# Dense expert layers: the share is applied by ScalarE on eviction, VectorE sums one tile later

## What is computed

```python
logits = jnp.einsum('bsd,de->bse', x, Wr)
w, sel = jax.lax.top_k(logits, 2)
w = jax.nn.softmax(w, axis=-1)
gate = jnp.einsum('bsk,bske->bse', w, jax.nn.one_hot(sel, E, dtype=w.dtype))
for e in range(E):          # E = 8, every expert for every token
    out = out + gate[..., e:e + 1] * (jnp.einsum('bsd,df->bsf', x, We[e]) + be[e])
# x = x + 0.5 * that, of layernorm(x)
```

## Time and profile before

| | us |
|---|---|
| median of 3 runs | 1696.71 (1686.7 to 1700.94) |
| span of the profiled execution | 1695.7 |
| dense layer 0, from its first row addition to its last sum | 963 to 1135 |
| dense layer 1, from its first statistics to its last sum | 1570 to 1693 |

### The profile page before, as it was taken

One profiled execution on the slowest core, in us unless ns is written; L12 is line 12 of the kernel. 1 busy time (PEld: TensorE's weight loads), 2 busy tenths in 40 slices (PEclk: granted clock), 3 DMA queues, 4 the chain that ended last, 5 costly groups with the idle time before them and its releaser, 6 DMA issues. The chain is left out here.

```text
span 1695.7 us, 39494 instructions
## 1 busy us (share of the span) xinstructions
PE 1441.4 (85%) x14334; PEld 990.9 (58%) x14334; DVE 1075.4 (63%) x2743; ACT 750.3 (44%) x1786; POOL 773.8 (46%) x741
## 2 busy tenths in 40 slices
PE   6879999448889996888999478877899999998799
PEld 3556656414545554455566356654677777777687
DVE  6852222457876564783222388876998888874888
ACT  5533333254555633553333311125776666752322
POOL 4453332763320000454333466606998888973000
PEclk9989999569999998899999788888999999999899
DMA  8309995631110002514999232200000000000000
GB/s 265 98 14 267 284 266 150 204 96 38 38 38 1 1 1 67 152 40 123 280 296 259 73 87 84 78 4 13 3 16 3 12 7 3 16 3 3 10 19 22
DMA packets 92664, 145.50 MB, mean 86 GB/s; under 512 B 25032, under 2 KB 52528, under 8 KB 92512
## 3 DMA queue, kind: packets, MB, share of 16 engines
q1 hardware_dynamic: 62816, 93.06, 19.1%
q0 software_dynamic: 15360, 37.77, 7.7%
q10 hardware_dynamic: 14336, 12.59, 2.7%
HBM read 122.39 MB, written 18.87 MB: 83 GB/s over the span
## 5 line engine op out<-in xcount | busy, mean ns | idle before, releaser
L2298 POOL TENSOR_TENSOR sb_m_prob<-sb_m_prob,sb_m_rinv 128x512 f32<-128x512 f32 x256 | 260.1, 1041 | 44.6 <-DVE sb_m_rinv L2348 40.8
L1272 POOL DMA_INDIRECT sb_c_rows<-slot_rows,sb_slot x192 | 192.1, 1000 | 102.7 <-issue 51.2
L2228 ACT ACTIVATE sb_m_prob<-m_ps_s,sb_m_nmax 128x512 f32<-128x512 f32 x256 | 173.8, 683 | 125.8 <-DVE sb_m_nmax L2354 125.2
L1106 POOL DMA_INDIRECT e_xn<-xn_rows,sb_table x128 | 117.7, 920 | 209.6 <-PE e_ps_x L1184 197.2
L1255 DVE TENSOR_TENSOR sb_e_h<-sb_e_sg,e_ps_gu 96x176 f32<-96x176 f32 x128 | 42.6, 333 | 256.5 <-ACT sb_e_sg L1231 256.5
L1193 PE MATMUL e_ps_gu<-e_wgu,sb_e_xT 128*96 128x352 f32 x512 | 178.1, 470 | 17.0 <-ACT sb_e_xT L1225 15.6
L2354 DVE TENSOR_REDUCE sb_m_nmax<-m_ps_s 128x1 f32<-128x512 f32 x256 | 163.8, 681 | 28.1 <-PE m_ps_s L2132 25.7
L2362 DVE STREAM_TRANSPOSE sb_m_pT<-sb_m_prob 128x1024 f32<-128x1024 f32 x128 | 157.5, 1232 | 0.0
L2145 PE MATMUL m_ps_v<-sb_m_pT,sb_m_lat_rows 32*64 32x128 f32 x8192 | 136.1, 275 | 4.6 <-issue 3.8
L2131 PE MATMUL m_ps_s<-sb_m_latT_high,sb_m_qa 128*128 128x512 f32 x256 | 125.5, 490 | 16.0 <-ACT sb_m_prob L2228 15.9
L2145 PEld LDWEIGHTS m_ps_v<-sb_m_pT,sb_m_lat_rows 32*64 32x64 f32 x8192 | 120.2, 131 | 27.8 <-issue 27.4
(11 more groups left out here) (280 smaller groups left out, 3076.4 us busy)
## 6 DMA issues: line engine op xcount, KB each, us to landing
e_wgu<-wgu SPq DMA_DIRECT2D x128, 352.0 KB, 4.9
e_wdn<-wdn SPq DMA_DIRECT2D x128, 192.0 KB, 4.7
slot_rows<-sb_e_y ACTq DMA_DIRECT2D x128, 96.0 KB
xn_rows<-e_xn SPq DMA_DIRECT2D x16, 256.0 KB, 2.2
sb_c_rows<-slot_rows,sb_slot POOLq DMA_INDIRECT x192, 2.8
sb_x<-x SPq DMA_DIRECT2D x4, 512.0 KB, 5.4
e_xn<-xn_rows,sb_table POOLq DMA_INDIRECT x128, 5.3
sb_g_zm<-wqT SPq DMA_DIRECT2D x1, 2048.0 KB, 9.1
```

Of the source, the lines that this page charges most:

```text
L1106: pool.indirect_dma_start(x, None, k.xn_rows[:, :], bass.IndirectOffsetOnAxis(ap=k.table[:, e:e + 1], axis=0))\
L1272: pool.indirect_dma_start(rows[u][j][:, :], None, k.slot_rows[:, :], bass.IndirectOffsetOnAxis(ap=k.slot[:, n, j:j + 1], axis=0))\
L2228: act.activation(prob[s % 4][:, hh, :], ps_s[j % 3][:, :], ACT.Exp, bias=nmax[s % 2][:, hh:hh + 1], accum_out=rsum[s % 2][:, hh:hh + 1]).t ...
L2298: pool.tensor_tensor(part, part, rinv[s % 2][:, hh:hh + 1].to_broadcast([P, T]), ALU.mult)\
```

## The change

The eight expert outputs of a tile are read by ACT instead of DVE. Each is a Copy with the token's share as a scale operand, into one of two buffers `gy[u]` of eight rows of 256 columns (`weigh`, two instructions per pair). ACT's `weigh(n, 0)` now stands first in its tile and waits for `gate_ready`; `inverse_deviation(n+2)` moves behind `weigh(n, 1)`. DVE no longer reads `ps_e`. In tile n it sums the eight rows of tile n-1 by halves (`halve` over 1024, 512 and 256 columns), adds the result to `x` (`add_up`), and adds the bias product of tile n from PSUM to `x` (`add_bias`), which ACT no longer copies. Before the gate of tile n is written, DVE waits until ACT has used up the gate of tile n-2. PE's bias matmul waits for `bias_added`. The last tile is summed after the loop. The loop starts at n = 2, with tiles 0 and 1 written out. The store of a tile waits for one more count of `out_ready`.

```diff
+        gy = [sb(f"d{r}_gated{u}", [P, 2 * NP, D]) for u in range(2)]
...
                 pe.wait_ge(gateT_ready, g + 1)
+                pe.wait_ge(bias_added, g + 1)
                 pe.matmul(ps_b[:, :], gateT[:, :], k.be1[:, :], start=True, stop=True).then_inc(bias_ready, 1)
...
+            def weigh(n, u, j):
+                g = n + r * NT
+                act.wait_ge(pair_ready, g * NP + (j + 1))
+                if j == 0:
+                    act.wait_ge(gate_ready, g + 1)
+                    act.wait_ge(out_ready, g + 1)
+                for i in range(2):
+                    ins = act.activation(gy[u][:, i * NP + j, :], ps_e[j][:, i, :], ACT.Copy,
+                                         scale=gate[u][:, 2 * j + i:2 * j + i + 1])
+                ins.then_inc(pair_free, 1)
...
             def tile(n, u):
                 g = n + r * NT
+                weigh(n, u, 0)
                 if live(n + 1):
                     copies(n + 1, 1 - u)
+                act.wait_ge(gateT_raw, g + 1)
+                act.activation(gateT[:, :], ps_g[:, :], ACT.Copy).then_inc(gateT_ready, 1)
+                weigh(n, u, 1)
                 if live(n + 2):
                     inverse_deviation(n + 2, u)
-                act.wait_ge(gateT_raw, g + 1)
-                act.activation(gateT[:, :], ps_g[:, :], ACT.Copy).then_inc(gateT_ready, 1)
-                act.wait_ge(bias_ready, g + 1)
-                act.wait_ge(out_ready, g + 1)
-                act.activation(acc[:, :], ps_b[:, :], ACT.Copy).then_inc(k.sem("d_bias_copied"), 1)
                 if live(n + 1):
                     gap_exp(n + 1)
+                weigh(n, u, 2)
+                weigh(n, u, 3)
...
+            def halve(n, u, width):
+                g = n + r * NT
+                if width == NP:
+                    dve.wait_ge(pair_free, g * NP + 2 * NP)
+                else:
+                    dve.wait_ge(halved, g * 3 + (1 if width == 2 else 2))
+                part = gy[u][:, 0:width, :]
+                dve.tensor_tensor(part, part, gy[u][:, width:2 * width, :], ALU.add).then_inc(halved, 1)
...
+            def add_bias(n):
+                dve.wait_ge(bias_ready, g + 1)
+                dve.tensor_tensor(x, ps_b[:, :], x, ALU.add).then_inc(bias_added, 1)
+
+            def add_up(n, u):
+                dve.wait_ge(halved, g * 3 + 3)
+                dve.wait_ge(bias_added, g + 2)
+                dve.tensor_tensor(x, gy[u][:, 0, :], x, ALU.add).then_inc(out_ready, 1)
+
+            def tile(n, u):
+                before = not isinstance(n, int) or n > 0
                 add(n + 3, 1 - u, 0)
                 if live(n + 2):
                     normalise(n + 2, u)
                 add(n + 3, 1 - u, 1)
+                if before:
+                    halve(n - 1, 1 - u, 4)
+                add(n + 3, 1 - u, 2)
+                if before:
+                    halve(n - 1, 1 - u, 2)
                 if live(n + 1):
                     leaders(n + 1, 1 - u)
+                if before:
+                    halve(n - 1, 1 - u, 1)
                 add(n + 3, 1 - u, 3)
...
+                rest = [last_sum, lambda: add(n + 3, 1 - u, 4), lambda: add_bias(n), lambda: add(n + 3, 1 - u, 5)]
                 if live(n + 1):
                     gates(n + 1, 1 - u, rest)
...
+            def last_tile_summed():
+                n, u = NT - 1, (NT - 1) % 2
+                for width in (4, 2, 1):
+                    halve(n, u, width)
+                add_up(n, u)
```

## The result

The changed kernel takes 1722.18 us (median; 1713.32 to 1725.81) beside 1694.12 for the kernel before, four runs each: 1.0145 times as long, with a 95% interval of 1.0101 to 1.019. The prediction was 1717 us with a range of 1700 to 1737; of its three cases slower, above 1713.7, came true. The profiled execution after has a span of 1724.0 us, before 1695.7.

The account below looks back on a forecast made before the run. ACT and DVE working in turn were to bound the dense tiles: 18.7 for dense layer 1 plus 4.6 for two ends less 2.6 for tile 0 gives +20.7, so 1717 us; range 1700 to 1737, copy and wait bounds 1706 to 1732.

Parts of the forecast that it names:

- slower: Whole kernel: measured time above 1713.7 us, one of three cases beside same and faster; chance 0.55.
- the ring: Dense layers: ACT and DVE wait for each other in turn each tile; 8.36 us in layer 1 against 6.92; chance 0.62.
- ACT's part: Dense layer 1, from `weigh(n, 0)` to the start of `normalise`: copies, gate's copy, second weighing pair, logarithm onward; 2.73 us.
- the weighing copies at 0.36: ACT's 256-column copies with per-token scale operand: 0.36 us from start to start, bounds 0.28 and 0.48.
- DVE's part: Dense layer 1, from `normalise` through halvings, `leaders` and `gates` until ACT sees the gate write; 5.45 us.
- The 0.06 for a place with several waits: Added in us at each of `weigh(n, 0)`, `add_up` and the gate write; between nothing and 0.12 each, 0.18 in all.
- The sum for dense layer 1: Thirteen tiles (n = 1 to 13) of dense layer 1, each 1.44 us longer: 18.7 us more.
- Dense layer 0: Five row additions inside add 1.48 us, so its tile stays 9.84 us; bounds 9.5 and 10.3.
- The ends: From last matmul to last sum of each dense layer: 3.78 us instead of 1.45, 2.3 more in each.
- The clock in dense layer 1: Rival, chance 0.15: PE's granted clock falls in dense layer 1 too, tile 9.84 us, 19 us more, 1736 us.
- That dense layer 0 could gain: Rival, chance 0.10: PSUM freed earlier, dense layer 0's tile 9.1 us instead of 9.84 on 12 tiles, 1708 us.
- the open ring: Rival, chance 0.13: ACT finds gates written early, PE runs without holes, dense layer 0 gains 0.77 us a tile; 1690 us.

Follow-up runs that it names:

- two orders: Two separate edits of the changed kernel: inverse_deviation(n+2) ahead of the gate's copy, 1698.6 us; normalise(n+2) behind leaders(n+1), 1690.0 us.
- a third one: Changed kernel with DVE's halving of four rows moved ahead of the first row addition and normalise(n+2); 1698.51 us, dense layer 1 tile 7.26.
- the same instruction: Changed kernel plus one idle 256-column DVE addition: between second halving and leaders, 1729.52 us; or behind the statistics, where DVE waits for ACT, 1724.46 us.
- the constant scale: Changed kernel with weighing copies scaled by constant 0.125 instead of the share's column of the gate buffer; 1714.08 us, dense layer 1 tile 8.17.
- the kernels of the table: The kernel before, 1694.12 us, the changed kernel, 1722.18 us, and the experiments' edits of the changed one, from 1679.77 to 1729.52 us.
- the late `normalise`: Changed kernel with DVE's normalise(n+2) behind leaders(n+1) instead of first in its tile; 1690.0 us, ratio 0.9955 to the kernel before.
- the last experiment: Row additions spread between other DVE work, against the kernel with late normalise, halving first and last four experts added from PSUM by DVE; 1679.77 us, ratio 0.9919.

## Why the prediction was right

**The mechanism** held: the ring closed in both layers, and cost 1.6 us a tile in dense layer 1, while in dense layer 0 it ate what DVE had saved. It is shown from four sides. In dense layer 1 two orders that loosen it on ACT's side and open it on DVE's gave back 0.89 and 1.61 a tile, a third one 1.25, and the same instruction cost 0.40 inside it and 0.05 outside.

**ACT's part, and the weighing copies at 0.36,** were right. In the turn above the gate write to `normalise` takes 1632.65 - 1629.67 = 2.98; the terms were 2.73, 0.20 for the gate write and 0.06 for the waits at `weigh(n, 0)`, 2.99 (for the gate's copy, 0.26 less 0.10 would have been 0.16 and not 0.17; it took 0.15). The two copies of a pair last 0.84 together and 0.478 each, so the second starts 0.36 behind the first. The reading behind that term was not right, though: the row of 690 ns in the earlier trace rows is another function, and its pointer is a bias (`ACT.Abs`, `bias=k.bgk1[...]`), not a scale. What a pointer as the scale costs, the constant scale alone shows; that it came to the same 0.09 was luck. The estimate by the Trainium skill (ScalarE: Activation LUTs, What ACT_TABLE_LOAD costs) was 0.40; the pointer operand's 93 ns agree with the 0.09 measured, the overlap is 0.12 here and not 93 ns.

**DVE's part** was 0.10 short in that tile, 5.37 from `normalise` to the gate write with the waits: 1638.12 - 1632.65 = 5.47. `normalise` took the 0.33, the two halvings 1.86 (1.87 predicted), `leaders` 1.22 (1.13), the third halving 0.34, the gates 1.72 (1.70 with the waits). So `leaders` was mis-sized, and little else. The 0.06 for a place with several waits stood in no row; in this tile `weigh(n, 0)` shows 0.05 and `add_up` 0.06. Of the loop's two bodies only one takes these 8.45; the other takes 8.65. There `normalise` starts 0.36 behind ACT's exponential instead of 0.23, and `add_up` 0.24 behind the first step of the gates instead of 0.12. For `normalise` I had priced no such wait, and `add_up` lost 0.18 where I had put 0.06 and 0.12 at the most. Why the two bodies differ is open. The mean of twelve tiles is 0.15 above my ring, 1.8 us in all.

**The sum for dense layer 1** was 18.7, from 13 tiles. Measured from the first gate to the fifteenth it is 22.4. Of the 3.7 more, half is the tile's size, and 1.8 come from tiles 0 and 1, which lost 3.25 instead of 1.44. I had said that PE sets tile 0 and had not followed the first tiles one by one. The profile shows PE late there: from the first gate to the second its granted clock was 0.67, before 0.92, and in tile 1 `weigh(n, 0)` started 1.19 us behind the gate, waiting for PE, instead of 0.25. That the change brings this about isn't shown; the first tile took from 7.14 to 9.89 us in the kernels of the table.

**Dense layer 0** was to keep its 9.84; it took 10.10. That term failed by 0.26, and most of it is `leaders` once more: 1.34 from its first row to the next instruction there. Its conversion of the index takes 0.30 where dense layer 1 has 0.17, and I had taken the price from dense layer 1. With twelve tiles 3.1 us more; tile 0 gave 2.8 back (2.6 predicted), and from the fourteenth gate to the last sum 1.7 were lost, where the end was to cost 2.3.

**The ends** were 3.78 in the sum and are 3.77. In dense layer 0 the old end was 1.81 and not the 1.45 of dense layer 1 that I had taken for both, so only 2.0 were lost in it.

**The rivals.** The ring stayed closed. The clock in dense layer 1 went from 0.96 to 0.94, but between the fourth gate and the fifteenth it was 1.00, before and after, and the tile is the ring's sum without it. That dense layer 0 could gain was half right: the change as made gave nothing, but with the ring open its tile is 9.2 and then 8.7. Of the saving on DVE that I had reckoned for the open ring, 0.77 a tile, the late `normalise` set free 0.64.

**The size.** The prediction was +20.7 us for the two layers, and 26.8 are measured; 3.8 of the rest are dense layer 1's, 2.3 dense layer 0's. The bounds of the copies and of the waits, added up, reach from 1704 to 1735 and not from 1706 to 1732; the result lies within both.

## What to carry to other kernels

Before moving work from a busy engine to an idle one, write down for each queue what stands behind its new wait, and follow it round: if the way comes back to where it began, the tile can't be shorter than the sum of the way, however idle all engines are. Such a ring was loosened here by order alone, by putting what the other engine waits for ahead of the new work (8.51 to 7.62), and opened by putting the consumer behind work that is ready (6.90). And when an instruction is moved to cover a wait, ask what it covered where it stood.

## What I had not expected of the hardware

Two DVE instructions had different durations in different places. The conversion of two indices took 301 ns in the mean between 1004 and 1104 of the kernel after and 169 between 1604 and 1704:

```profile
L444 DVE CAST sb_d_top_f<-sb_d_top_i 128x2 f32<-128x2 uint32 x9 | 2.7, 301 | 0.0
```
```profile
L444 DVE CAST sb_d_top_f<-sb_d_top_i 128x2 f32<-128x2 uint32 x12 | 2.0, 169 | 0.0
```

`normalise` took 412 in both layers of that kernel, 587 in dense layer 0 with the constant scale, and 0.53 us in dense layer 0 of the last experiment, where in turn the conversion was back at 0.17. The halvings over 1024 columns took 1.19 to 1.23 us everywhere. POOL's gathers run in dense layer 0 alone, and the traces tie the long ones to them, here with the constant scale:

```profile
1060.41 0.95 POOL L1291 DMA_INDIRECT sb_c_rows<-slot_rows,sb_slot  x1 [0.30 <-issue]
1060.91 0.56 DVE L427 TENSOR_SCALAR sb_d_xn<-sb_x,sb_d_mv,sb_d_rstd 128x256 f32 x1 [0.57 <-ACT sb_d_rstd L341]
...
1064.24 0.97 POOL L1291 DMA_INDIRECT sb_c_rows<-slot_rows,sb_slot  x1 [0.30 <-issue]
1064.89 0.30 DVE L444 CAST sb_d_top_f<-sb_d_top_i 128x2 f32<-128x2 uint32 x1
```

The conversion ends with the gather (1065.19 and 1065.21), `normalise` 0.11 behind it (1061.47 and 1061.36). It is so in dense layer 0 of all eleven traces: each of the 92 conversions above 0.2 us started while a gather was running, at most 0.43 us before its end, and ended with it, within 0.02; each of the 39 `normalise` above 0.44 us ended 0.11 to 0.12 behind one. The 84 short conversions started with no gather running or earlier in one. So an instruction's place in the order decides whether it meets the end of a gather. That is read from the times; no kernel without the gathers was run.

The granted clock of dense layer 0 rose from 0.85 to 0.91 with the change, and over 1004 to 1104 from 0.86 to 1.00, while its tile grew by 0.26 us. PE worked 74 us of those 100 instead of 83. So the mean clock was no measure of the tile there.
